# A decoder layer with a delta-rule attention on one Trainium2 core: a counted loop over heads written out

## What is computed

```
qkv = x @ W_qkv.T ; z = x @ W_z.T            # 16 key heads, 2 value heads for each, width 128
beta = sigmoid(x @ W_b.T)
decay = exp(-softplus(x @ W_a.T + dt_bias) * exp(A_log))
q, k, v = causal 4-tap convolution of qkv over time, split by head ; k = k / |k|
for each token t:                            # state: 128 x 128 for each value head
    delta = (v_t - k_t . state) * beta_t
    state = state * decay_t + k_t (x) delta
    o_t   = q_t . state
y = (rmsnorm(o) * silu(z)) @ W_out.T
x = x + y
```

## Time and profile before

| what | us |
|---|---|
| median of three runs | 4343.22 |
| lowest and highest of them | 4336.3 and 4344.09 |
| the profiled execution, its own time | 4339.26 |
| its span, from the first instruction to the last | 4337.5 |
| TensorE busy in the span | 3928.8 |
| VectorE busy | 2995.1 |
| ScalarE busy | 2443.1 |

### The profile page before, as it was taken

One profiled execution on the slowest core, in us unless ns is written; L12 is line 12 of the kernel. 1 busy time (PEld: TensorE's weight loads), 2 busy tenths in 40 slices (PEclk: granted clock), 3 DMA queues, 4 the chain that ended last, 5 costly groups with the idle time before them and its releaser, 6 DMA issues. The chain is left out here.

```text
span 4337.5 us, 75366 instructions
## 1 busy us (share of the span) xinstructions
PE 3928.8 (91%) x26288; PEld 2913.2 (67%) x26288; DVE 2995.1 (69%) x5082; ACT 2443.1 (56%) x4829; POOL 545.4 (13%) x445
## 2 busy tenths in 40 slices
PE   3899999999999999999999999984988988299998
PEld 2677777777777777777777777762444444188887
DVE  3788888887888888878888888864655554722222
ACT  2677667676777676766767677761544445211111
POOL 0000000000000000000000000002333332311110
PEclk7999999999999999999999999996999999699999
DMA  2010111010101110101001010105556552100001
GB/s 76 15 42 27 33 36 33 26 42 16 43 26 33 35 33 26 42 17 43 26 32 37 16 43 26 33 8 85 90 80 96 84 94 35 44 20 20 20 15 39
DMA packets 133895, 171.97 MB, mean 40 GB/s; under 512 B 12508, under 2 KB 79836, under 8 KB 132988
## 3 DMA queue, kind: packets, MB, share of 16 engines
q1 hardware_dynamic: 131068, 165.84, 16.3%
q10 hardware_dynamic: 2432, 1.05, 0.2%
HBM read 142.92 MB, written 21.76 MB: 38 GB/s over the span
## 5 line engine op out<-in xcount | busy, mean ns | idle before, releaser
L407 PE MATMUL pj<-xh,w_hi 128*128 128x512 f32 x1536 | 684.4, 446 | 16.8 <-DVE w_lo L746 16.5
L407 PE MATMUL pj<-xh,w_lo 128*128 128x512 f32 x1536 | 607.8, 396 | 0.0
L407 PE MATMUL pj<-xl,w_hi 128*128 128x512 f32 x1536 | 600.9, 391 | 0.0
L1572 DVE TENSOR_REDUCE row_max<-s 128x1 f32<-128x512 f32 x512 | 342.4, 687 | 272.9 <-PE s L1326 269.7
L1057 POOL TENSOR_TENSOR silu_z<-silu_z,exp_z 128x512 f32<-128x512 f32 x128 | 185.3, 1469 | 2641.1 <-ACT exp_z L633 2641.1
L1506 ACT ACTIVATE probs<-s 128x512 f32<-128x512 f32 x512 | 291.4, 595 | 325.2 <-PE s L1350 319.4
L407 PEld LDWEIGHTS pj<-xh,w_hi 128*128 128x128 f32 x1536 | 291.1, 190 | 65.7 <-DVE w_lo L746 17.0
L407 PEld LDWEIGHTS pj<-xh,w_lo 128*128 128x128 f32 x1536 | 288.8, 188 | 66.2
L407 PEld LDWEIGHTS pj<-xl,w_hi 128*128 128x128 f32 x1536 | 292.2, 190 | 50.2 <-issue 14.8
L1350 PE MATMUL s<-q_stack,k_stack 128*128 128x512 f32 x512 | 249.0, 489 | 75.2 <-DMA q_stack<-row_maxima 67.2
L812 DVE SCALAR_TENSOR_TENSOR conv_v<-conv_in,conv_w_section,conv_v 128x512 f32<-128x512 f32 x384 | 288.0, 750 | 10.7 <-ACT conv_v L616 1.6
(11 more groups left out here) (258 smaller groups left out, 9887.4 us busy)
## 6 DMA issues: line engine op xcount, KB each, us to landing
w_raw<-in_w_in SPq DMA_DIRECT2D x128, 256.0 KB, 6.2
decays<-decay_by_head SPq DMA_DIRECT2D x64, 512.0 KB, 3.8
decays<-decay_by_head SPq DMA_DIRECT2D x64, 256.0 KB, 5.1
q_stack<-qk_parts SPq DMA_DIRECT2D x128, 128.0 KB
k_stack<-qk_parts SPq DMA_DIRECT2D x128, 128.0 KB
f_raw<-in_f_w SPq DMA_DIRECT2D x32, 256.0 KB, 2.6
x_all<-in_x SPq DMA_DIRECT2D x4, 1024.0 KB, 10.3
source<-in_ctx SPq DMA_DIRECT2D x8, 512.0 KB
```

The source lines that it names most:

```text
L407: mm = pe.matmul(pj[j % 2][:, :], a[:, j, k * P:(k + 1) * P], b[:, k, bp * WIN:(bp + 1) * WIN], start=(n == 0), stop=(n == 3 * KT - 1))
L1572: dve.reduce_max(mx[g % 2][:, i:i + 1], s1[n % 2][:, :], AX_X).then_inc(E["rm"].sem, 1)
```

## The change

In `run`, the head loop on the chip is replaced by a Python loop, so that the code of all sixteen heads stands in a row in the streams of TensorE, ScalarE and VectorE, each with constant head numbers. The functions that it calls, the flags of the first and last head, and the streams of SyncE and GpSimd are as they were.

```diff
             prologue(eng)
-            head(0, True, False)
-            with eng.Fori(1, HK - 1) as hk:
-                head(hk, False, False)
-            head(HK - 1, False, True)
+            for hk in range(HK):
+                head(hk, hk == 0, hk == HK - 1)
             epilogue(eng, Section(HK - 1, NSEC - 1), HK - 1)
```

## The result

The changed kernel took 4304.93 us (median of four runs, 4300.76 to 4307.86) against 4340.64 us before (four runs, 4336.3 to 4344.09). The ratio is 0.9918, with a 95% interval of 0.99 to 0.9935: about 0.8% faster. 4308 was forecast, within 4301 to 4321. A second measurement of the same kernel gave 0.9921 (0.9907 to 0.9934).

A forecast was written before the change was run, and what follows sets the result against it. The head loop was taken to run at TensorE's speed, plus 2.45 us per jump back: 4339.26 - 31.9 (13 jumps) = 4307.4 us, with register work and straight code at nothing; stated as 4308 us, range 4301 to 4321.

The forecast's parts named there:

- What bounds a head: Delta stage: heads run at TensorE's speed; a loop head takes 175.38 us against 172.93 without a jump, 2.45 us more.
- The cause is the jump: Delta stage's head loop: removing the 13 jumps back, 2.45 us each, saves 31.9 us.
- Register work costs nothing: Head loop's semaphore targets, offsets and loop arithmetic: hidden under queued matmuls, costed at nothing, at most 1.7 us extra gain.
- How the sum is made up over the engines: At the jumps: 31.9 us exceeds TensorE's own 12.4 us because TensorE then waits for late VectorE and ScalarE.
- Only TensorE's wait goes: Rival, chance 0.04: VectorE and ScalarE keep a stall at the head's start; only 12.4 us gained, 4326.9 us.
- Straight code runs without stops: Written-out heads: block crossings costed at nothing; a fetch that comes too late costs at most 2.45 us.
- The slower rival: Chance 0.04: fetches in straight code come too late, 2.45 us each; two a head give 4376 us.
- A later loop starts to stall: Rival, chance 0.06: the moved cross attention loop pays 5 x 2.45 = 12.3 us, giving 4319.7 us.
- Busy times stay: Sign in the profile after: VectorE's, ScalarE's and TensorE's busy times stay as before.
- The stages behind: Stages after the delta stage: unchanged, starting 32 us earlier; more than a few microseconds longer would count against the prediction.

The follow-up runs named there:

- two_heads_a_pass: Changed kernel with heads 1 to 14 again in a loop, two heads in its body, so 6 jumps back instead of 13: 4322.05 us, ratio to before 0.9959.
- loop_scalar_vector: Changed kernel with ScalarE and VectorE keeping the loop of before and TensorE written out: 4325.48 us (one run).
- loop_tensor_only: Changed kernel with only TensorE keeping the loop of before, ScalarE and VectorE written out: 4342.71 us (one run).
- cross_two_batches: Changed kernel with two batches in the body of the cross attention's loop, 2 jumps instead of 5: 4315.78 us, ratio to before 0.9944.

## Why the prediction was right

*What bounds a head.* Right. The difference between a head of the loop and a head with constants, read from the kernel before, was the whole effect: 31.9 us forecast, 32.2 measured over the same 13 heads. The comparison of like windows carried the prediction; it needed no theory of the stall, and so it came out although part of the theory was wrong.

*The cause is the jump.* Right, and shown by two_heads_a_pass: in one kernel, with the same register work in every head, the heads with a jump behind them take 174.9 us and those without 173.0.

*Register work costs nothing.* Nearly right. Heads with register work and no jump take 173.03 us in the mean of two_heads_a_pass, heads with constants 172.90. That is 0.13 us a head or 1.7 us in 13, the prediction's upper bound. The sum hardly felt it: 32.2 us measured against 31.9.

*How the sum is made up over the engines.* Wrong, in the sentence "It is larger than TensorE's 12.4 us alone, because after its own stall TensorE waits for what VectorE and ScalarE deliver late". TensorE's loop alone pays 2.60 us a head, 34 us in all, of which half is a second stop of its own at line 448. It comes from the place of the body: 64 transposes of padding in the source (128 instructions in the stream) take it away. Only then do the other two engines show behind TensorE: 1.62 us a head for all three against 1.31 for TensorE alone. The rival "Only TensorE's wait goes" gave 12.4 us; the run in that state, loop_scalar_vector, gains 14.2 us over the heads and took 4325.48 us against the rival's 4326.9. So its number was good, by the overlap of stops, while 12.4 us is not what TensorE's jump costs. The sum was not hurt, since it was a difference of whole heads, and all three jumps went. Had the change been made on ScalarE and VectorE only, I would have forecast a gain, and loop_tensor_only says there is none.

*Straight code runs without stops.* Right: heads 1 to 14 each took between 172.8 and 173.0 us. In them 146 packets came in on queue 8, TensorE's, and no matmul waited for issue. The slower rival did not come about.

*A later loop starts to stall.* It did not happen here; the jumps of the cross attention cost no wait for issue after the change. cross_two_batches shows that the danger is real once a body is long. It also shows that 2.45 us, the price this rival took for a jump and the bound that the prediction put on a late fetch, is not the dearest: ScalarE's two waits were 7.4 and 8.4 us, and the kernel was 11 us slower with two jumps.

*Busy times stay.* Not for VectorE: 12.4 us more over the 13 heads, beside GpSimd's products, at no cost in time.

*The stages behind.* "Unchanged" was right within their own spread (1544.7 us before, 1539.7 and 1547.0 after). The measured 35.7 us are 3.8 more than the sum; the interval of the ratio (28 to 43 us) holds both.

The rule of the Trainium skill on taken branches (Runtime: NRT & Kernel Launch, section Instruction fetch mechanics) agrees with these runs: 67 ns for the branch that falls through, 3618 for the one taken. The room that the same section gives ScalarE and VectorE, 512 instructions, does not decide it: with 380 and 458 instructions a pass in the trace before, they do wait at their jumps, 25.3 and 28.3 us in all where they alone loop.

## What to carry to other kernels

Before a loop on the chip is judged, compare one pass of it with the same work written out, if the kernel has a first or last pass with constants: windows between like marks give the price of the jump to a few hundredths of a microsecond. Look for waits for issue whose count is the number of jumps, and for packets of instructions that come in on each pass; a short body that draws none has no such stop to lose (whether writing it out gains a few microseconds in another way is open here), and a loop whose body no longer stays on the chip is written out. Here that had to be done on all three engines for the whole gain: TensorE alone gave 14.2 of the 32.2 us, ScalarE and VectorE without TensorE gave nothing. Padding ahead of a loop is a cheap probe of whether the place of its body costs time. And before a run counts as a test of register work, its count of instructions tells whether the work is in it.

## What the runs showed of the hardware

A jump back to code that has to come in can stop an engine twice, once at the jump and once some 26 instructions later, with one packet of instructions in each stop. On TensorE the two cost 2.60 us a head and one 1.31 us, in the same code moved by 128 instructions. That the second comes from a body that starts close to the end of a block is the reading that fits.

ScalarE's stop was far longer in a stage full of transfers: 7.4 and 8.4 us in the cross attention (DMA share 0.63 at the first), against at most 2.4 us in the delta stage. The traffic is the likely cause, not a shown one.

A loop body of 857 instructions on TensorE, and one of 1712, jumped back in some 0.2 us (215 ns in the median for the branch); the delta stage's body of 2797 took 3.6 us. ScalarE's body of 234 instructions was held, those of 380 and 466 were not.

TensorE's branch record of 3.6 us is longer than its idle time of 1.0 us at the same place, because matmuls are still queued when its sequencer stops: in loop_tensor_only the branch runs from 468.7 to 472.4 us, and matmuls of line 582 still start at 471.2.
